# A graph-network layer on one core: GpSimd may fill three pairs of the gather ring ahead in place of four

## The chip, the core and the metric

The kernel runs on one core of a Trainium2 chip. A core has five engines that run side by side, each with its own queue of instructions: TensorE (PE), VectorE (DVE), ScalarE (ACT), GpSimd (POOL) and SyncE (SP, which only starts transfers here), and 16 DMA engines. The metric is device time in microseconds; lower is better.

## What is computed

There are 6250 nodes with 128 values each and 106250 edges, sorted by the node that they lead to. Each edge carries 64 values and one weight. Biases and names are cut to what matters:

```
ef  = relu(edge_attr @ We1 + be1) @ We2 + be2
ef  = ef * sigmoid(edge_weight * Wt + bt)
msg = relu(concat(x[src], ef) @ Wn1 + bn1) @ Wn2 + bn2
out = segment_sum(msg, dst) + x
y   = layernorm(x + out)
```

## The kernel before

**Table.** x[src] @ Wn1[:128] + bn1 needs no edge, so the kernel first makes a table `node_table` of x @ Wn1[:128] + bn1 in DRAM, block by block (13 blocks), and later gathers its rows in place of x's. A gather is an indirect DMA that GpSimd issues: 128 rows of 512 bytes, one for each partition.

**Edges.** 512 edges (4 tiles of 128) are a group, two groups a pair, two pairs a super. There are 104 pairs, numbered from 0. The last matrix product with Wn2 is made after the sum over a node's edges, so each edge costs: a transpose of its attributes (L767), two products (L803, L815), ScalarE's sigmoid (L591) and relu (L599), VectorE's product of the two (L1090), the product with Wn1[128:] (L790), VectorE's addition of the gathered rows (`pre`, L1069), a relu (L535), and a product with a one-hot matrix of the destination nodes (L748) whose result is added to `acc` at L1033.

**Steps.** Each engine works in steps. Step s holds the transposes of pair s, the second layer of pair s - 1, the addition of the gathered rows to pair s - 2 (MSG_LAG), the sums of pair s - 3, and the accumulation of pair s - 4. Some steps also finish a block of 512 nodes (product with Wn2, layer norm, store).

**Gathers.** The rows of pairs 0 to 3 (RAW = 8 groups) are gathered from x itself before the table exists, 32 gathers, into buffers of their own. All later pairs, 4 to 103, use the ring `gathered`: BODY = 4 slots, one pair each, pair p in slot p % 4, eight gathers for each pair, 800 in all. GpSimd starts them once the source ids are spread (`src_e_ready`) and the whole table has landed (`wait_table`, L485). A slot may be filled again when the pair in it has been added: VectorE raises `pre_ready` by one at each addition (L1109). GpSimd runs nothing but these gathers in the main part; its order is the loop at L486. VectorE waits for a pair's landing at L1108, and TensorE at L867 (called at L798, ahead of L803), which makes it wait for the first six gathers of pair s - 2. The last pair's gathers signal one tile at a time (L495), so that its additions can follow each landing.

**Ids.** Pair 7 is the fourth and last pair that fits into the ring before any has been added; pair 8 is the first that must wait at L488.

Of the kernel before, what the change touches and what calls it, by code (L numbers as in the profile page):

```python
# [57 lines left out]
PAIR = 2  # L58
PE2 = PAIR * GE
EF_LAG, MSG_LAG, H_LAG, SUM_LAG, ADD_LAG, SUPER_LAG = 1, 2, 3, 3, 4, 6  # L60
RAW, RAW_BEFORE = 8, 4
# [14 lines left out]
def gnn_kernel(nc, x, src, dst, edge_attr, edge_weight, We1, be1, We2, be2, Wt, bt, Wn1, bn1, Wn2, bn2, out):  # L76
# [6 lines left out]
    BODY = 4  # L83
# [20 lines left out]
    with ExitStack() as ctx:  # L104
# [6 lines left out]
        def sem(name):  # L111
            return ctx.enter_context(nc.semaphore(name))
# [106 lines left out]
        ef_ps, efw_ready, msg_ps, pre_ready, h_ready = (  # L219
            sem(n) for n in ("ef_ps", "efw_ready", "msg_ps", "pre_ready", "h_ready"))  # L220
# [55 lines left out]
        def wait_table(eng):  # L276

            for r, n in enumerate((RING, RING, len(BLOCKS) - 2 * RING)):
                eng.wait_ge(table_out[r], 16 * n)
# [184 lines left out]
        @block.gpsimd  # L464
        def _(pool):
            pool.memset(ident[:, :], 0.0).then_inc(ident_ready, 1)
            pool.wait_ge(ident_ready, 1)
            pool.affine_select(out=ident[:, :], in_=ident[:, :], compare_op=ALU.not_equal, fill=1.0,
                               base=0, pattern=[[-1, P]], channel_multiplier=1).then_inc(ident_ready, 1)
            pool.iota(window_ids[:, :], pattern=[[1, W]], base=0, channel_multiplier=0,  # L470
                      allow_small_or_imprecise_dtypes=True).then_inc(window_ids_ready, 1)
            pool.iota(split_ids[:, :, :], pattern=[[IDS, W1 // IDS], [1, IDS + 1]], base=0, channel_multiplier=0,
                      allow_small_or_imprecise_dtypes=True).then_inc(window_ids_ready, 1)
            pool.memset(zero_c[:, :], 0.0).then_inc(zero_ready, 1)

            def gather_rows(to, rows, index, landed):
                pool.indirect_dma_start(to, None, rows, bass.IndirectOffsetOnAxis(index, 0)).then_inc(landed, 16)  # L477

            for g in range(RAW):
                if g % 2 == 0 and g <= SG:  # L480
                    pool.wait_ge(raw_e_in[g // 2], 16)
                for t in range(TILES):
                    gather_rows(raw_rows[g][:, t * C:(t + 1) * C], x, raw_e[:, g, ORDER[t]:ORDER[t] + 1], raw_in[g])
            pool.wait_ge(src_e_ready, 2)
            wait_table(pool)  # L485
            for p in range(RAW // PAIR, PAIRS):  # L486
                if p >= RAW // PAIR + BODY:
                    pool.wait_ge(pre_ready, p - (BODY - 1))  # L488
                    pool.nop(nofuse=True)
                for q in range(PAIR):  # L490
                    for t in range(TILES):
                        if p < PAIRS - 1:
                            landed = gather_in[p % BODY][0 if q * TILES + t < PART[0] else 1]
                        else:
                            landed = last_gather_in[0 if q == 0 else 1 + t]  # L495
                        gather_rows(gathered[:, p % BODY * PAIR + q, t * C:(t + 1) * C], table,
                                    src_e[:, p * PAIR + q, t:t + 1], landed)
# [901 lines left out]
```

## Time and profile before

| | |
|---|---|
| median of 3 runs | 1063.79 us (1063.65 to 1064.85) |
| span of the profiled execution | 1405.6 us |
| GpSimd busy in it | 787.6 us, 56% |
| TensorE busy in it | 975.4 us, 69% |
| VectorE, ScalarE busy | 651.4 and 582.0 us |
| gathers of the table | 800, 945 ns each on average |

The profile shows one execution, taken while the hardware profiler recorded it. Its span is 32% longer than the timed runs; no separate time of that execution is given besides its span. The page lists for each engine how long it was busy, and for waits what ended them. "remote" and "another core or an unknown queue" mean that the profile has no record of what released the waiting instruction. "issue" means that the engine waited for nothing that the profile shows. A gather's record on GpSimd is the making of its descriptors, not the moving of the data.

### The profile page before, as it was taken

How to read it: one execution, taken by the hardware profiler on the slowest of the kernel's cores; microseconds unless marked ns; L12 is line 12 of the kernel's file. 1: busy time of each engine (PE TensorE's matmuls, PEld its weight loads, DVE VectorE, ACT ScalarE, POOL GpSimd, SP SyncE). 2: the span in 40 equal slices, each digit the busy share in tenths (PEclk: the TensorE clock that was granted, in tenths of full speed). 3: DMA queues.
4: the chain of work that ended last, by engine and by line, in shares of the span. 5: the costliest groups of instructions: out<-in, count | busy, mean ns of one | idle time of the engine just before them, and what ended most of it. 6: DMA issues, size and time to landing. Idle time of an engine off the chain costs nothing.

```text
span 1405.6 us, 15476 instructions
## 1 busy us (share of the span) xinstructions
PE 975.4 (69%) x5031; PEld 704.8 (50%) x5032; DVE 651.4 (46%) x1688; ACT 582.0 (41%) x649; POOL 787.6 (56%) x841
## 2 busy tenths in 40 slices
PE   3547777686776767577578667678576857685775
PEld 3535455454555446455355545555454535453554
DVE  1425444445345445355345534545444535444446
ACT  1325434444444435344244443444344433442442
POOL 7270456655665565566566556556555656655640
PEclk8768978888798888789789888789788888887887
DMA  6433242333323324233242332433323324333310
GB/s 187 144 111 116 85 133 89 124 95 107 120 86 109 116 93 134 87 108 123 85 135 86 109 113 90 124 98 109 118 86 100 126 87 133 96 107 106 98 33 19
DMA packets 70435, 148.44 MB, mean 106 GB/s; under 512 B 17511, under 2 KB 45350, under 8 KB 63686
## 3 DMA queue, kind: packets, MB, share of 16 engines
q1 hardware_dynamic: 41126, 89.26, 18.7%
q0 software_dynamic: 26624, 54.58, 13.6%
q10 hardware_dynamic: 2592, 3.48, 0.7%
q8 instruction: 45, 0.74, 0.2%
q14 instruction: 48, 0.39, 0.1%
HBM read 140.85 MB, written 6.40 MB: 105 GB/s over the span
## 4 chain that ended last, share of the span: by engine, by line
PE 35%; another core or an unknown queue 29%; ACT 19%; issue 12%; DVE 3%; ACTq 1%; DMA 0%; DVEq 0%; SPq 0%
PE psS L748 11%; PE psM L790 8%; ACT tw L591 7%; PE psH L803 7%; PE psE L815 5%; ACT h L535 4%; ACT h L599 2%; ACT eaT L567 1%; ACT found L532 1%; ACT x_sb L612 1%; DVE efw L1090 1%; ACT staged_own L627 1%; PE psS L733 1%; PE psT L767 1%
## 5 line engine op out<-in xcount | busy, mean ns | idle before, releaser
L477 POOL DMA_INDIRECT gathered<-node_table,src_e x800 | 756.2, 945 | 563.8 <-DVE h L1069 284.0
L748 PE MATMUL psS<-onehot,h 128*128 128x128 f32 x1656 | 269.1, 329 | 180.2 <-ACT h L535 154.2
L599 ACT ACTIVATE h<-psH,be_c 128x1024 f32<-128x1024 f32 x104 | 115.8, 1114 | 615.3 <-remote 374.6
L748 PEld LDWEIGHTS psS<-onehot,h 128*128 128x128 f32 x1656 | 251.0, 239 | 199.3 <-issue 126.7
L1069 DVE TENSOR_TENSOR h<-psM,gathered 128x1024 f32<-128x1024 f32 (+1 forms) x104 | 122.7, 1182 | 475.5 <-remote 388.5
L815 PE MATMUL psE<-h,we 128*128 128x512 f32 x416 | 235.3, 687 | 16.4 <-issue 16.1
L790 PE MATMUL psM<-wn,efw 128*128 128x128 f32 x1664 | 227.4, 293 | 21.7 <-issue 15.8
L591 ACT ACTIVATE tw<-ew,bt_c,wt_c 128x1024 f32<-128x1024 f32 x104 | 234.0, 2251 | 7.8 <-DVE efw L1090 3.9
L790 PEld LDWEIGHTS psM<-wn,efw 128*128 128x128 f32 x1664 | 219.0, 211 | 16.1 <-issue 9.7
L1090 DVE SCALAR_TENSOR_TENSOR efw<-psE,be_c,tw 128x1024 f32<-128x1024 f32 x104 | 133.2, 1281 | 127.3 <-PE psE L815 80.3
L803 PE MATMUL psH<-eaT,we 64*128 64x512 f32 x416 | 150.1, 692 | 52.0 <-issue 51.8
L1075 DVE TENSOR_SCALAR onehot<-split_ids,dst_e 128x65 f32<-128x65 f32 x832 | 173.8, 271 | 0.0
L815 PEld LDWEIGHTS psE<-h,we 128*128 128x128 f32 x416 | 79.2, 210 | 164.6 <-issue 164.5
L535 ACT ACTIVATE h<-h 128x1024 f32<-128x1024 f32 (+1 forms) x108 | 110.5, 1026 | 9.9 <-DVE h L1069 9.4
L1083 DVE TENSOR_REDUCE found<-onehot 128x128 f32<-128x512 f32 x104 | 109.8, 1055 | 9.6 <-remote 5.7
L567 ACT ACTIVATE eaT<-psT 128x512 f32<-128x512 f32 x104 | 61.7, 593 | 107.0 <-remote 77.2
L767 PEld LDWEIGHTS psT<-ident,ea 128*128 128x128 f32 x416 | 56.6, 151 | 78.3 <-issue 78.3
L803 PEld LDWEIGHTS psH<-eaT,we 64*128 64x128 f32 x416 | 41.2, 195 | 84.9 <-issue 74.5
L1033 DVE TENSOR_TENSOR acc<-acc,found 128x128 f32 x204 | 58.1, 285 | 48.1 <-issue 31.9
L767 PE MATMUL psT<-ident,ea 128*128 128x128 f32 x416 | 69.5, 288 | 14.8 <-issue 14.8
L733 PE MATMUL psS<-wn,staged_own 128*128 128x128 f32 x88 | 23.0, 351 | 75.2 <-ACT h L535 44.9
L733 PEld LDWEIGHTS psS<-wn,staged_own 128*128 128x128 f32 x88 | 16.6, 236 | 80.6 <-issue 80.6
(111 smaller groups left out, 357.1 us busy)
## 6 DMA issues: line engine op xcount, KB each, us to landing
ew<-in_edge_weight SPq DMA_DIRECT2D x52, 1024.0 KB
ea<-in_edge_attr SPq DMA_DIRECT2D x52, 512.0 KB
gathered<-node_table,src_e POOLq DMA_INDIRECT x800
x_sb<-in_x SPq DMA_DIRECT2D x6, 512.0 KB, 6.3
out_y<-x_sb ACTq DMA_DIRECT2D x12, 256.0 KB
node_table<-gathered SPq DMA_DIRECT2D x7, 256.0 KB, 2.0
node_table<-h SPq DMA_DIRECT2D x4, 256.0 KB
h<-in_x,raw_e POOLq DMA_INDIRECT x16
```

What stands on the lines that cost most here:

```text
L477: pool.indirect_dma_start(to, None, rows, bass.IndirectOffsetOnAxis(index, 0)).then_inc(landed, 16)
L535: return nc.scalar.activation(at, at, ACT.Relu)
L591: nc.scalar.activation(tw[:, s % 2, :].rearrange("c (o i m) -> c o i m", o=2, i=2), ew[s // 2 % 2][:, s % 2 * PAIR:(s % 2 + 1) * PAIR, :] ...
L599: nc.scalar.activation(h1[:, s % 2, :], psH[:, :, :].rearrange("p r e -> p (r e)"), ACT.Relu, bias=be1_c[:, :]).then_inc(h1_ready, 1)
L748: return nc.tensor.matmul(to, h[:, (k - SUM_LAG) % BODY * PAIR + q, t * C:(t + 1) * C], hot, start=(t == 0), stop=(t == TILES - 1))
L767: mm = nc.tensor.transpose(psT[:, (a * PAIR + q) * P:(a * PAIR + q + 1) * P], ea[k // 2][:, k % 2 * PAIR + q, a * P:(a + 1) * P], ident[:, :])
L790: mm = nc.tensor.matmul(psM[:, q, t * P:(t + 1) * P], efw[:, (k - MSG_LAG) % 2, of], wn1[:, 1, :], start=True, stop=True)
L803: mm = nc.tensor.matmul(psH[:, a, :], we1[a * F:(a + 1) * F, :], eaT[a * F:(a + 1) * F, k % 2, :], start=True, stop=True)
L815: mm = nc.tensor.matmul(psE[:, r, :], we2[:, :], h1[:, (k - EF_LAG) % 2, r * GE:(r + 1) * GE], start=True, stop=True)
L1069: return nc.vector.tensor_tensor(to, of, rows, ALU.add)
L1075: made = nc.vector.tensor_scalar(onehot[:, (k - MSG_LAG) % 2, q * TILES + t, :].rearrange("p (a b) -> p a b", b=IDS), split_ids[:, :, 0:ID ...
L1090: nc.vector.scalar_tensor_tensor(efw[:, (k - EF_LAG) % 2, :], psE[:, :, :].rearrange("p r e -> p (r e)"), be2_c[:, :], tw[:, (k - EF_LAG) ...
```

## The change

GpSimd may gather a pair's rows once the pair three in front of it has been added, in place of four. The ring keeps its four slots; one of them less is filled ahead. The first pair that waits is 7 in place of 8.

```
             for p in range(RAW // PAIR, PAIRS):
-                if p >= RAW // PAIR + BODY:
-                    pool.wait_ge(pre_ready, p - (BODY - 1))
+                if p >= RAW // PAIR + BODY - 1:
+                    pool.wait_ge(pre_ready, p - (BODY - 2))
                     pool.nop(nofuse=True)
                 for q in range(PAIR):
                     for t in range(TILES):
```

## Rows read from the trace of the kernel before

**Rows 1.** The page: span, busy us with share and instructions, the chain that ended last.

```profile
span 1405.6 us, 15476 instructions
PE 975.4 (69%) x5031; PEld 704.8 (50%) x5032; DVE 651.4 (46%) x1688; ACT 582.0 (41%) x649; POOL 787.6 (56%) x841
...
by line: another core or an unknown queue 28.7%; issue 12.0%; PE psS L748 10.7%; PE psM L790 8.0%; ACT tw L591 7.4%; PE psH L803 7.0%; PE psE L815 5.2%; ACT h L535 4.5%; ACT h L599 1.8%; ACT eaT L567 1.2%; ACT found L532 1.1%; ACT x_sb L612
```

**Rows 2.** Waits, whole span: engine, line, releaser: us in total, times, longest.

```profile
DVE h L1069 <- remote: 407.9, 68, 19.4
...
POOL gathered L477 <- DVE h L1069: 284.0, 60, 41.8
```

**Rows 3.** GpSimd's gathers: ns min/median/max, first and last start in us.

```profile
L477 POOL DMA_INDIRECT gathered<-node_table,src_e x800: 938/944/1096, 67.3 to 1361.9; - x160
```

**Rows 4.** Timeline, GpSimd: start us, us, instruction, [idle before <- releaser].

```profile
3.10 1.10 POOL L477 DMA_INDIRECT h<-in_x,raw_e  x1 [1.19 <-DMA raw_e<-in_src]
...
41.96 0.94 POOL L477 DMA_INDIRECT raw_own<-in_x,raw_e  x1 [0.30 <-issue]
67.25 0.94 POOL L477 DMA_INDIRECT gathered<-node_table,src_e  x1 [24.36 <-DMA node_table<-gathered]
68.50 0.94 POOL L477 DMA_INDIRECT gathered<-node_table,src_e  x1 [0.30 <-issue]
...
105.95 0.94 POOL L477 DMA_INDIRECT gathered<-node_table,src_e  x1 [0.30 <-issue]
148.73 0.94 POOL L477 DMA_INDIRECT gathered<-node_table,src_e  x1 [41.84 <-DVE h L1069]
```

**Rows 5.** Windows: us, busy of each engine, granted clock, DMA share, GB/s.

```profile
125.00:157.00 32.00, 30.93 (x183) 21.48 (x184) 20.73 (x51) 20.52 (x20) 6.44 (x7) 1.00 0.38 132
148.00:1363.00 1215.00, 867.57 (x4408) 617.72 (x4407) 566.54 (x1468) 518.66 (x563) 725.96 (x768) 0.83 0.33 105
1363.00:1364.00 1.00, 0.00 (x0) 0.00 (x0) 0.00 (x0) 0.88 (x1) 0.00 (x0) 1.00 0.23 66
1364.00:1365.00 1.00, 0.00 (x0) 0.00 (x0) 0.43 (x1) 1.00 (x4) 0.00 (x0) 1.00 0.00 0
```

**Rows 6.** Timeline, the last additions of gathered tiles.

```profile
1391.53 0.48 DVE L1069 TENSOR_TENSOR h<-psM,gathered 128x128 f32<-128x128 f32 x2
```

**Rows 7.** The chain in order of time, to 150 us: start us, us, what.

```profile
13.85 4.72 issue
...
21.78 7.28 another core or an unknown queue
...
30.17 17.82 another core or an unknown queue
...
78.57 5.66 another core or an unknown queue
...
89.18 2.74 another core or an unknown queue
91.97 20.34 another core or an unknown queue
112.34 0.24 DVE h L1069
```

**Rows 8.** Timeline, VectorE: additions to pairs 1 to 4.

```profile
122.18 1.23 DVE L1069 TENSOR_TENSOR h<-psM,h 128x1024 f32<-128x1024 f32 x1 [0.70 <-PE psM L790]
...
131.78 1.21 DVE L1069 TENSOR_TENSOR h<-psM,raw_own 128x1024 f32<-128x1024 f32 x1
...
138.97 1.23 DVE L1069 TENSOR_TENSOR h<-psM,raw_own 128x1024 f32<-128x1024 f32 x1 [0.36 <-PE psM L790]
...
146.76 1.22 DVE L1069 TENSOR_TENSOR h<-psM,gathered 128x1024 f32<-128x1024 f32 x1 [0.52 <-PE psM L790]
```

**Rows 9.** Timeline, VectorE: two additions in the main part.

```profile
1114.47 1.22 DVE L1069 TENSOR_TENSOR h<-psM,gathered 128x1024 f32<-128x1024 f32 x1 [0.18 <-issue]
...
1134.16 1.22 DVE L1069 TENSOR_TENSOR h<-psM,gathered 128x1024 f32<-128x1024 f32 x1 [12.44 <-remote]
```

## Prediction

> **What bounds the kernel now.** I read the page's span and busy table first, then the waits, then GpSimd's instructions in order of time, then the chain. The reader is to see that they do not agree at first sight. No engine is full: TensorE is busy for 69% of the span and GpSimd for 56% [rows 1]. In the waits GpSimd stands 284.0 us in front of L477 until VectorE's add at L1069 releases it, so in the profiled execution it looks like an engine with room to spare. But the largest wait of all, VectorE's 407.9 us at that same add, ends in "remote", work that the profile doesn't name [rows 2], and 29% of the chain that ended last is of that kind [rows 1]. The profiled span is 1405.6 us where the median of the timed runs is 1063.79 us, 341.8 us less. So I do not take the span as the timed run. I ask which engine could still need 1063.8 us once those unnamed waits are gone.
>
> The chain without them is 1405.6 x (1 - 0.287) = 1002 us [rows 1], less than was measured. VectorE, ScalarE and TensorE together, as the chain runs through them, would be done earlier than 1063.8.
>
> GpSimd is different. Its 800 gathers of the table take a median of 944 ns each [rows 3], and the next starts 0.30 us after one has ended; from 67.25 to 105.95 there are 31 pitches [rows 4], 38.70 / 31 = 1.249 us with the rounding of the starts. The 32 raw ones have it too: 3.10 to 41.96, 31 pitches and a slower first one. A pair is eight gathers, 10.0 us. If it never waited, it would start at 3.10 and be done with 832 at 3.1 + 832 x 1.249 = 1042 us. Behind it come the landing of the last rows and the end of the kernel. The DMA engines still move 66 GB/s in the microsecond 1363 to 1364 and nothing in the next, with the last gather's record over at 1361.9 + 0.94 = 1362.8 [rows 3, 5]: 1.2 us. The last two tiles are added from 1391.53 on, and the span ends at 1405.6 [rows 6]: 14.1 us. Together 1042 + 15.3 = 1057.6 us, within 6.2 us of the measured 1063.79. Of the two candidates only GpSimd's issue fills the timed run, and it leaves 6 us for everything else that it waits for. I conclude that the timed kernel is bound by GpSimd's gathers nearly from its start to its end.
>
> **Where GpSimd still waits, and how long.** Twice at the start. It is done with the 32 raw gathers at 42.90 and waits for the table until 67.25 (24.36 us), then fills four pairs of the ring until 106.9 and waits 41.84 us for the first of them to be added, until 148.73 [rows 4]. Both waits lie behind unnamed pieces of the chain: 7.28 and 17.82 us ahead of the table; 5.66, 2.74 and 20.34 us behind it [rows 7]. Taken out, the table is ready at 67.25 - 25.1 = 42.2, so GpSimd goes on as soon as it is free, at some 43.2. Four pairs take it to 43.2 + 32 x 1.249 = 83.2. The first addition of a gathered pair releases it at 148.73 - 53.8 = 94.9, or at 90.2 if the 4.72 us "issue" piece goes too [rows 7]. From there 96 pairs are left: 94.9 + 96 x 8 x 1.249 + 15.3 = 1069.4, or 1064.7 from 90.2. The measured time asks for a release at 1063.8 - 959.2 - 15.3 = 89.3. I take 89.3 to 95, so before the change the wait on the full ring is 6 to 12 us long, not 41.84.
>
> This is the place that decides, so I work out its lower end from the other side. The additions of pairs 1 to 4 start at 122.18, 131.78, 138.97 and 146.76, the last two steps (7.2 and 7.8 us) with TensorE at full granted clock (1.00 over 125 to 157, busy 30.93 of 32 us) [rows 5, 8]. They can't be packed closer. From the table to the addition of pair 0 there are 112.34 - 67.25 = 45.1 us with 28.7 us unnamed, so 16.4 us of named work; then 35.6 us to the end of pair 4's addition (146.76 + 1.22 - 112.34) and 0.8 us to the gather. 42.2 + 16.4 + 35.6 + 0.8 = 95.0. Even if three of the four steps between them were as short as 7.2 us, that is some 6 us less, 89.
>
> **The change, part by part.**
> 1. The test and the number waited for in L487 and L488. For p = 8 to 103 the wait is on a count higher by one; p = 7 waits where it didn't. One more wait instruction of GpSimd's queue: free against a 10 us pair. Nothing but gathers is queued behind it on GpSimd.
> 2. Pair 7's eight gathers move from before the first wait to behind it. Their issue, 8 x 1.249 = 9.99 us, was made while GpSimd would otherwise have stood waiting (83.2 is already their end); the cover was the wait on pair 4. Now three pairs are filled by 43.2 + 24 x 1.249 = 73.2, GpSimd stands until the same 89.3 to 95, and has 97 pairs ahead of it instead of 96. What is late next is each later pair's landing, by one pair. Cost: +9.99 us, if the release at 89.3 or later is past 83.2.
> 3. Slack behind the wait. VectorE at L1069 and TensorE at L799 need pair 7 three steps after the addition of pair 4. Three steps of 7.2 to 9.6 us are 22 to 29 us [rows 8]; eight gathers and their landing are 11.2 us. So nobody waits for pair 7 itself. The consumers then gain about 2.5 us a step on GpSimd (10.0 less 7.5) and catch up with it, after which they wait on landings for the rest.
> 4. The shorter ring in the steady part. GpSimd would be held by it only if a pair's addition came later than two pairs (20 us) after its gathers ended, where it was three pairs (30 us). The widest distance between additions that I saw is 1134.16 - 1114.47 = 19.7 us, and 12.44 us of it are an unnamed wait [rows 9]; without that it is 7.3 us. I count nothing here; the upper bound is below.
> 5. Less traffic before the first addition: 8 gathers of 64 KB move behind it. The bound on both sides: TensorE at full clock has no wait on a transfer in rows 8, so 0; if one of its pieces did depend on it, the 0.5 to 0.7 us waits ahead of those additions are the gain.
>
> Sum against the profiled execution: its consumers are held by the unnamed waits, so its GpSimd waits anyway, and its span should stay near 1405.6, with only the first wait longer by 10 us. Sum against the timed median: 1063.8 + 10.0 = 1073.8 us, +0.94%.
>
> A rule of the skill speaks against this. The rows show GpSimd's track broken by 284.0 us of waits for VectorE and busy for 56% [rows 1, 2]. The Trainium skill, page "Perfetto Trace Analysis", section "What "DMA-bound" means", calls a kernel bound by the DMA sequencer when the issuing engine's track is solid with DMA slices, which it is not here; by that rule an issue slot moved behind a wait would cost nothing, and the sum would be 1063.8. The same skill, page "Trainium Kernel Development and Optimization", section "Best Practices", asks for two buffers to cover transfers, which three slots would satisfy. Both would be right for the profiled execution.
>
> **The rivals.**
> - A, not slower: GpSimd isn't the bound of the timed runs; place: the whole main loop; price 0; time 1063.8. It decides if the consumers need over 8 x 1.249 = 10.0 us a pair in the timed run, or if the gathers' pitch there is below what the consumers' chain needs, (1002 - 95 - 15) / 96 = 9.3 us a pair, 1.16 us a gather. For it: the waits of rows 2, and a mean granted clock below full in the main loop (0.83) [rows 5]. Against it: the consumers' chain is 62 us short of the measured time, GpSimd's only 6 us. Chance 0.14.
> - B, part of it: the release comes before the fourth pair is filled, at 74 to 83; then the loss is the release less 73.2, 1 to 9 us, 1065 to 1072.8. Against it: the lower end worked out above. 0.06.
> - C, more than a slot: the ring of three also holds GpSimd in the steady part. Some steps carry the finishing of a block of nodes (12 of them); if in the timed runs two of them reach past 20 us, each holds GpSimd by some 5 us: 1084. 0.08.
> - D, the change doesn't act or helps: the earlier additions come sooner by the 0.5 to 0.7 us of part 5 and nothing else moves. It would need A as well. Below 1061.7. 0.02.
> - Forecast: one pair's issue, 1073 to 1074.8. 0.70.
>
> **How the numbers follow.** The likeliest is the forecast, 1073.8. About 0.2% (2.1 us) is what a measurement of this kernel can tell from no change. Slower by more: forecast, C and nearly all of B, 0.83. Within it: A and a small part of B, 0.15. Faster: D, 0.02. The range takes in A, B and the forecast with a pitch of 1.16 to 1.264 us (9.3 to 10.1 us a pair) and 2 us for unlike releases: 1063.5 to 1076.
>
> **What would show it.** In the changed kernel's profile: the first ring wait of GpSimd starts after 24 gathers of the table, not 32, and is about 52 us, not 41.84; eight gathers of pair 7 follow the addition of pair 4; the pitch stays 1.25 us; the profiled span stays within some 1% of 1405.6. Step 2 is wrong if the timed runs gain much less than 10 us; then the release came early or GpSimd was not the bound. Step 4 is wrong if they lose over 12 us.

## The result and the profile after

The changed kernel takes 1075.55 us (median; 1072.32 to 1077.79) where the kernel before takes 1064.32 us in the same runs. The ratio is 1.0097, with a 95% interval of 1.0082 to 1.0112. It is slower, by 8.7 to 11.9 us. The forecast was 1073.8 us, +0.94%.

The profiled execution of the changed kernel has nothing of the unnamed waits that filled the one of before. Its span is 1070.5 us, close to the timed runs. The page, its span, its busy table and how the chain that ended last divides:

```profile
span 1070.5 us, 15477 instructions
PE 865.2 (81%) x5031; PEld 628.6 (59%) x5032; DVE 649.8 (61%) x1688; ACT 588.2 (55%) x649; POOL 788.5 (74%) x841
...
POOL 61%; issue 22%; DMA 5%; PE 5%; DVE 4%; ACT 2%; SPq 1%; DVEq 0%; ACTq 0%; POOLq 0%
```

In [rows 1] 29% of the chain was unnamed and TensorE's lines led it. Here GpSimd's gathers are 61% of it, and "issue", mostly the 0.30 us between two gathers, is 22%: the bound that the prediction argued for can be read off directly. GpSimd is busy for 74% and not 100% because those 0.30 us are not counted as busy.

The waits of the same kernel, in the columns of [rows 2]:

```profile
POOL gathered L477 <- issue: 241.4, 792, 0.3
DVE h L1069 <- DMA gathered<-node_table,src_e: 198.3, 66, 7.1
...
POOL gathered L477 <- DVE h L1069: 14.1, 8, 12.0
```

The roles of [rows 2] have changed over. GpSimd stood 284.0 us in front of L477 there, and 14.1 us here, of which one wait is 12.0. VectorE waited for something unnamed there; here it waits 198.3 us for gathers to land, 66 times. The 792 pauses of at most 0.3 us are the fixed distance between gathers.

GpSimd's timeline around its one wait, and two additions of VectorE in the main part:

```profile
72.30 0.94 POOL L477 DMA_INDIRECT gathered<-node_table,src_e  x1 [0.30 <-issue]
85.24 0.94 POOL L477 DMA_INDIRECT gathered<-node_table,src_e  x1 [12.00 <-DVE h L1069]
86.49 0.94 POOL L477 DMA_INDIRECT gathered<-node_table,src_e  x1 [0.30 <-issue]
```

```profile
706.70 1.23 DVE L1069 TENSOR_TENSOR h<-psM,gathered 128x1024 f32<-128x1024 f32 x1 [2.83 <-DMA gathered<-node_table,src_e]
...
718.76 1.23 DVE L1069 TENSOR_TENSOR h<-psM,gathered 128x1024 f32<-128x1024 f32 x1 [5.68 <-DMA gathered<-node_table,src_e]
```

The 24th gather of the table ends at 73.2, and the next starts at 85.24. In [rows 4] it was the 32nd that ended at 106.9, and 148.73 that released the next. But that profile can't be set against this one line by line, since its consumers were held up by waits that are not here. The first experiment gives a profile of the kernel before that can.

### The profile page after: what moved, and what is told of

It reads as the page before. It is cut to its first block, busy times and chain, and to the rows that moved or that the text cites. A ratio compares the mean times of both kernels' runs of the same rounds, so it can differ in the third digit from the quotient of the medians.

```text
span 1070.5 us, 15477 instructions
## 1 busy us (share of the span) xinstructions
PE 865.2 (81%) x5031; PEld 628.6 (59%) x5032; DVE 649.8 (61%) x1688; ACT 588.2 (55%) x649; POOL 788.5 (74%) x841
## 4 chain that ended last, share of the span: by engine, by line
POOL 61%; issue 22%; DMA 5%; PE 5%; DVE 4%; ACT 2%; SPq 1%; DVEq 0%; ACTq 0%; POOLq 0%
POOL gathered L477 61%; DMA gathered<-node_table,src_e 3%; PE psS L748 2%; PE psM L790 1%; DVE h L1069 1%; DMA x_sb<-in_x 1%; DMA ew<-in_edge_weight 1%; ACT tw L591 1%; ACT h L535 1%; PE psH L803 0%; DVE onehot L1075 0%; SPq L400 0%; DVE gathered L943 0%; SPq L406 0%; ACT x_sb L612 0%
## 5 line engine op out<-in xcount | busy, mean ns | idle before, releaser
L477 POOL DMA_INDIRECT gathered<-node_table,src_e x800 | 756.7, 946 | 255.5 <-issue 241.4
L748 PE MATMUL psS<-onehot,h 128*128 128x128 f32 x1656 | 233.5, 298 | 79.8 <-ACT h L535 77.3
L1069 DVE TENSOR_TENSOR h<-psM,gathered 128x1024 f32<-128x1024 f32 (+1 forms) x104 | 122.8, 1183 | 255.8 <-DMA gathered<-node_table,src_e 198.3
L748 PEld LDWEIGHTS psS<-onehot,h 128*128 128x128 f32 x1656 | 215.6, 209 | 98.7 <-issue 52.3
L815 PE MATMUL psE<-h,we 128*128 128x512 f32 x416 | 217.9, 648 | 0.0
L790 PE MATMUL psM<-wn,efw 128*128 128x128 f32 x1664 | 212.4, 283 | 4.8 <-DVE h L1069 4.8
L790 PEld LDWEIGHTS psM<-wn,efw 128*128 128x128 f32 x1664 | 205.1, 201 | 5.6 <-DVE h L1069 5.6
L803 PE MATMUL psH<-eaT,we 64*128 64x512 f32 x416 | 123.6, 672 | 56.0 <-DMA gathered<-node_table,src_e 55.9
L815 PEld LDWEIGHTS psE<-h,we 128*128 128x128 f32 x416 | 74.0, 198 | 135.8 <-issue 135.8
L767 PEld LDWEIGHTS psT<-ident,ea 128*128 128x128 f32 x416 | 53.4, 145 | 56.8 <-issue 56.8
L803 PEld LDWEIGHTS psH<-eaT,we 64*128 64x128 f32 x416 | 32.5, 192 | 70.7 <-DMA gathered<-node_table,src_e 61.9
L767 PE MATMUL psT<-ident,ea 128*128 128x128 f32 x416 | 63.7, 277 | 0.2 <-DMA ea<-in_edge_attr 0.2
L733 PE MATMUL psS<-wn,staged_own 128*128 128x128 f32 x88 | 21.2, 327 | 40.8 <-ACT h L535 40.8
```

Source lines behind the costliest of these rows:

```text
L748: return nc.tensor.matmul(to, h[:, (k - SUM_LAG) % BODY * PAIR + q, t * C:(t + 1) * C], hot, start=(t == 0), stop=(t == TILES - 1))
L767: mm = nc.tensor.transpose(psT[:, (a * PAIR + q) * P:(a * PAIR + q + 1) * P], ea[k // 2][:, k % 2 * PAIR + q, a * P:(a + 1) * P], ident[:, :])
L790: mm = nc.tensor.matmul(psM[:, q, t * P:(t + 1) * P], efw[:, (k - MSG_LAG) % 2, of], wn1[:, 1, :], start=True, stop=True)
L803: mm = nc.tensor.matmul(psH[:, a, :], we1[a * F:(a + 1) * F, :], eaT[a * F:(a + 1) * F, k % 2, :], start=True, stop=True)
L815: mm = nc.tensor.matmul(psE[:, r, :], we2[:, :], h1[:, (k - EF_LAG) % 2, r * GE:(r + 1) * GE], start=True, stop=True)
L1069: return nc.vector.tensor_tensor(to, of, rows, ALU.add)
```

## Experiments

### The kernel before once more

No edit.

> The kernel before, unchanged, to see a profile of it without the unnamed waits. Theory (GpSimd's issue is the bound, its only ring wait is the first one): 1064 us; GpSimd starts the gathers of the table at some 43.6, has filled four pairs at 83.3, is released at some 85.2 as in the changed kernel's profile, so waits 2 us and not 41.84, and then issues 96 pairs at 10.0 us. Rival (the profiled execution of before is typical of the timed ones): a span near 1400 us in the profile again, and 60 waits of GpSimd for VectorE.

Measured: 1064.19 us, ratio to before 0.9996 (0.9983 to 1.0009), profiled span 1061.6 us. Its GpSimd timeline at the first wait, and its waits:

```profile
82.18 0.95 POOL L477 DMA_INDIRECT gathered<-node_table,src_e  x1 [0.30 <-issue]
84.89 0.94 POOL L477 DMA_INDIRECT gathered<-node_table,src_e  x1 [1.77 <-DVE h L1069]
86.14 0.94 POOL L477 DMA_INDIRECT gathered<-node_table,src_e  x1 [0.31 <-issue]
```

```profile
DVE h L1069 <- DMA gathered<-node_table,src_e: 197.7, 65, 5.6
...
POOL gathered L477 <- DVE h L1069: 3.9, 8, 1.8
```

This is the same place in the kernel before. GpSimd has filled four pairs at 83.1, waits 1.77 us, and is released at 84.89, 0.35 us from the 85.24 of the changed kernel. So the release did not move by more than that, and the one wait grew from 1.77 to 12.00 us: 10.23 us, of which eight pitches of 1.25 us are 10.0. The profile ahead of the prediction was of an exceptional execution. What held its engines in it stays open: of the ten profiles taken after it, of these kernels and of variants, none shows a wait that ends in "remote".

### Only the first wait

```
-                if p >= RAW // PAIR + BODY:
-                    pool.wait_ge(pre_ready, p - (BODY - 1))
+                if p >= RAW // PAIR + BODY - 1:
+                    pool.wait_ge(pre_ready, max(p - (BODY - 1), RAW // PAIR + 1))
```

> Only pair 7 waits for pair 4's addition; pairs 8 to 103 keep the wait on the pair four in front. Theory (the loss is pair 7's issue, moved out of the first wait): all of the loss, +8 to +10 us, about 1073 us, with a first wait of 12.0 us. Rival (the ring of three holds GpSimd in the steady part): less than the change loses, in the extreme 1064 us.

Measured: 1075.57 us, ratio 1.0083 (1.0056 to 1.0111), so +8.8 us by the ratio and +10.9 by the medians. Within these intervals that is the whole loss of the change, with the full depth of the ring for pairs 8 to 103. Its waits and its one long wait in the timeline:

```profile
POOL gathered L477 <- DVE h L1069: 13.8, 7, 12.0
```

```profile
85.59 0.94 POOL L477 DMA_INDIRECT gathered<-node_table,src_e  x1 [12.00 <-DVE h L1069]
```

### Only the later waits

```
                 if p >= RAW // PAIR + BODY:
-                    pool.wait_ge(pre_ready, p - (BODY - 1))
+                    pool.wait_ge(pre_ready, p - (BODY - 2))
```

> The other half: pair 7 is gathered freely as before, pairs 8 to 103 wait for the pair three in front. Theory: pair 8 then waits for pair 5's addition, which ends one step of 7.2 us later than pair 4's, so GpSimd is held at 83.3 until 92.4 in place of 85.2: +7.2 us, about 1071.5 us, with one wait of 9.2 us at the start and none to speak of later. Rival (the steady part costs nothing and neither does the start): 1064 us. Rival (the steady part costs by itself): over 1073 us, with waits spread over the main part.

Measured: 1071.03 us, ratio 1.0066 (1.0041 to 1.0090), so +7.0 us by the ratio and +6.4 by the medians, where +7.2 was worked out.

```profile
82.07 0.94 POOL L477 DMA_INDIRECT gathered<-node_table,src_e  x1 [0.30 <-issue]
92.50 0.94 POOL L477 DMA_INDIRECT gathered<-node_table,src_e  x1 [9.49 <-DVE h L1069]
```

```profile
POOL gathered L477 <- DVE h L1069: 12.2, 10, 9.5
```

Pair 8 now waits for pair 5, one step later: 92.50 in place of 84.89, 7.6 us. The total of all its waits for VectorE is 12.2 us, and 9.49 of it are this one. The ring of three costs nothing behind it. The two halves of the change lengthen the first wait by 10.2 and 7.7 us, but together by 10.2, not 17.9: both are the same wait, entered or left at different points. They can't be added.

### Two pairs ahead

```
-                if p >= RAW // PAIR + BODY:
-                    pool.wait_ge(pre_ready, p - (BODY - 1))
+                if p >= RAW // PAIR + BODY - 2:
+                    pool.wait_ge(pre_ready, p - (BODY - 3))
```

> One slot less again: GpSimd may gather a pair once the pair two in front has been added. Theory: the first wait begins after 16 gathers, at 63.3, and ends at the same 85.2, so 98 pairs are left: another +10.0 us over the changed kernel, about 1084 us, as long as a pair's addition ends within 10 us of the end of its gathers. Additions ended 2 to 8 us after it in the changed kernel's profile, so a few waits of 1 to 3 us may come on top: 1084 to 1100 us. Rival (the loss is a fixed price of the first wait or of the earlier wait instruction): about 1074 us.

Measured: 1085.52 us, ratio 1.0198 (1.0160 to 1.0235), +21.1 us by the ratio, +20.9 by the medians, and about twice the change's loss.

```profile
62.29 0.94 POOL L477 DMA_INDIRECT gathered<-node_table,src_e  x1 [0.30 <-issue]
86.23 0.94 POOL L477 DMA_INDIRECT gathered<-node_table,src_e  x1 [23.00 <-DVE h L1069]
```

```profile
POOL gathered L477 <- DVE h L1069: 28.5, 19, 23.0
```

A second slot costs a second pair's issue. The wait is 23.0 us: 20 us more than before are the issue of two pairs, and 1.3 us come from the release, which lies at 86.23 in this execution and not at 84.89. The 5.5 us that are left of 28.5 are spread over 18 others of 0.3 us each, the ordinary distance. Even a ring of two does not hold GpSimd in the main part.

The spans of the profiled executions follow from one sum. All five kernels issue 800 gathers of the table; they differ by the one wait:

| kernel | wait, us | wait less 1.77 | span less 1061.6 | timed median less before's |
|---|---|---|---|---|
| before, once more | 1.77 | | | -0.5 |
| changed | 12.00 | 10.2 | 8.9 | 11.2 |
| only pair 7 | 12.00 | 10.2 | 12.1 | 10.9 |
| only later | 9.49 | 7.7 | 7.2 | 6.4 |
| two ahead | 23.00 | 21.2 | 21.2 | 20.9 |

What is left between the wait and the span, up to 2 us, lies in the pitch and in the end of the kernel. Behind the wait the pitch is (1045.5 - 84.89) / 767 = 1.2524 us in the kernel before and (1054.5 - 85.24) / 775 = 1.2507 us in the changed one; 768 times the difference is 1.3 us. In the kernel with only pair 7 the last gather starts at 1056.7, which makes its pitch 1.2530 us, and its end, from that start on, is 17.0 us where the kernel before has 16.1.

```profile
L477 POOL DMA_INDIRECT gathered<-node_table,src_e x800: 940/944/1415, 43.5 to 1045.5; - x160
```

```profile
L477 POOL DMA_INDIRECT gathered<-node_table,src_e x800: 940/944/1397, 43.6 to 1054.5; - x160
```

The first row is of the kernel before, the second of the changed one.

### Fewer gathers: where is the next bound?

The number of gathers left out was put into the loop, and the counts that L1108 and L867 wait for were lowered with it:

```
+LEFT_OUT = 1
+LANDED = (PART[0] - LEFT_OUT, PART[1])
...
                     for t in range(TILES):
+                        if p < PAIRS - 1 and q * TILES + t < LEFT_OUT:
+                            continue
```

> The kernel before with one gather of each pair's eight left out for pairs 4 to 102 (the first tile of the even group, so its rows are stale), everything else the same. Theory (GpSimd's issue is the bound): four pairs are filled at 43.6 + 28 x 1.249 = 78.6, released at 85.2; (95 x 7 + 8) x 1.249 = 840.6 us of issue and 15.1 us of end follow: 941 us plus 2 us around the span. Rival A (the engines that use the rows are the bound): near 1064 us.

Measured: 950.34 us, ratio 0.8925 (0.8909 to 0.8941), 7 us above the 943 that the theory gave and 114 us below the kernel before. Of the kernel with one gather left out (its line numbers are 2 to 4 higher), GpSimd's gathers and the waits for them:

```profile
L479 POOL DMA_INDIRECT gathered<-node_table,src_e x701: 941/947/1348, 43.5 to 929.3; - x176
```

```profile
DVE h L1073 <- DMA gathered<-node_table,src_e: 26.5, 21, 4.8
POOL gathered L479 <- DVE h L1073: 11.7, 13, 8.0
```

GpSimd still waits only once for long, 8.0 us. The 99 gathers less are worth 99 x 1.25 = 124 us. Of the 10 us that were not gained, 6.3 lie in the first wait, 8.03 us in place of 1.77, since four of the gathers left out were issued ahead of it and the release came at 86.51. Another 3.5 lie in the end behind the last gather, which has grown from 15.2 to 948.9 - 929.3 - 0.9 = 18.7 us. And VectorE's waits for landings have shrunk from 198 us to 26.5: the consumers are now nearly as slow as the gathers. That the end is longer because the consumers are further behind is argued only.

The same with LEFT_OUT = 2:

> Two of each pair's eight gathers left out for pairs 4 to 102 (the first two tiles of the even group). GpSimd alone would need 85.2 + (95 x 6 + 8) x 1.249 + 15.1 = 822 us. TensorE's step took 7.2 to 7.8 us at full clock without the finishing of blocks, so its chain is 85 + 99 x 7.5 + 15 = 843 us and some 2 to 4 us more for each of 12 blocks: 870 to 890 us, and GpSimd should now wait for VectorE all through the main part. Theory: 860 to 900 us, bound by TensorE's chain. Rival: 1064 us if the gathers never were the bound, 824 us if TensorE's chain is shorter than I think.

Measured: 939.83 us, ratio 0.8828 (0.8813 to 0.8844). The bound has changed over, as the theory had it: no wait of VectorE for a landing is left, and TensorE leads the chain that ended last, where GpSimd had 63% of it in the kernel before:

```profile
PE 65%; ACT 12%; issue 9%; DVE 7%; DMA 3%; ACTq 2%; DVEq 1%; SPq 1%
```

But the time is 40 us above the 900 of the theory. My 7.5 us a step had left out that the steps are not alike; these additions follow each other at 7.2 to 10.6 us:

```profile
514.23 1.22 DVE L1073 TENSOR_TENSOR h<-psM,gathered 128x1024 f32<-128x1024 f32 x1
522.52 1.23 DVE L1073 TENSOR_TENSOR h<-psM,gathered 128x1024 f32<-128x1024 f32 x1 [2.87 <-PE psM L794]
529.74 1.23 DVE L1073 TENSOR_TENSOR h<-psM,gathered 128x1024 f32<-128x1024 f32 x1
536.97 1.22 DVE L1073 TENSOR_TENSOR h<-psM,gathered 128x1024 f32<-128x1024 f32 x1
547.59 1.22 DVE L1073 TENSOR_TENSOR h<-psM,gathered 128x1024 f32<-128x1024 f32 x1 [2.07 <-PE psM L794]
```

```profile
POOL gathered L479 <- DVE h L1073: 121.9, 59, 14.3
```

From 503.95 to 598.13 there are eleven steps in that timeline, 8.6 us each. The first ten steps after pair 4's addition take 7.4 us on average (85.69 to 159.91), and the eight from 529.74 to 598.13 take 68.4 us, some 9 us more than eight at that pace. One block of nodes is finished in them, its product with Wn2 in the two steps from 536.97 to 556.25, and 2 to 4 us had been expected for a block. That the block accounts for all of the 9 us is argued only.

And the same edit on top of the change, three pairs ahead:

> The same two gathers of each pair left out, with the change: three pairs ahead. Theory: GpSimd now has 2 us and more to spare in each pair, so pair 7's issue is hidden again and the change costs nothing: the time of the kernel with two left out, within 3 us. Rival (the change costs by the depth of the ring, whoever is the bound): slower by the issue of a pair, 7.5 us, or more.

Measured: 946.15 us (937.16 to 948.78, 4 runs), ratio 0.8901 (0.8879 to 0.8923). That is 6.3 us over its partner's median, outside the 3 us of the theory, and the two intervals do not overlap, so by these runs the rival was ahead; but the profiled spans stand the other way round, 935.4 us with three ahead and 943.2 us with four. The medians alone don't settle it, and I made another pair with more room for GpSimd.

LEFT_OUT = 3, four and three pairs ahead:

> The kernel before with three of each pair's eight gathers left out for pairs 4 to 102 (the first three tiles of the even group). GpSimd alone would need 85 + (95 x 5 + 8) x 1.249 + 15 = 703 us. Theory: with two left out TensorE's chain was already the bound at 940 us, so nothing more is gained: 935 to 942 us. Rival (the rows' traffic or GpSimd's issue still set the time with two left out): some 100 us less, 820 to 840 us.

> The same three gathers left out, with the change: three pairs ahead. Theory: the change costs nothing where GpSimd has room; the time of the kernel with three left out, within 3 us. Rival (the 6 us between the two kernels with two gathers left out are a real price of the shorter ring): 5 us or more slower again.

Measured: 941.12 us (ratio 0.8820, 0.8796 to 0.8844) with four ahead, 938.49 us (ratio 0.8808, 0.8784 to 0.8832) with three. The waits, first with four ahead, then with three:

```profile
POOL gathered L479 <- DVE h L1073: 253.5, 96, 16.8
```

```profile
POOL gathered L479 <- DVE h L1073: 256.2, 95, 24.1
```

A third gather less brought nothing (939.8 and 941.1 us), so the consumers' chain of some 940 us is the bound from there on, and not the rows' traffic. The change costs nothing there that these runs can tell, although the first wait is 7.3 us longer: 24.1 in place of 16.8. Pair 7's five gathers are 6.2 us of this, and a release 1.1 us later (86.03 and 84.97) is the rest. GpSimd has over 250 us of waits in which to give them back.

The 6 us of the pair before did not come back, and the granted clock of the single runs says where they lie. In the 22 runs of these four kernels the time goes with TensorE's mean granted clock:

| mean granted clock of the run | runs | time, us |
|---|---|---|
| 0.970 to 0.974 | 12 | 937.07 to 940.62 |
| 0.968 and 0.969 | 3 | 940.66 to 941.99 |
| 0.964 to 0.966 | 5 | 944.54 to 945.40 |
| 0.962 | 2 | 947.76 and 948.78 |

With two gathers left out, three of the four runs with three pairs ahead have 0.966 or less, and two of the six with four ahead. At the same clock the two agree: 944.54 us with three ahead and 945.13 us with four, both at 0.966; 937.16 and 938.25 us, both at 0.972. So at an equal clock no price of the shorter ring is seen. Why the clock differs from run to run is open, and four runs can't exclude that the change had a part in it there; with three gathers left out the kernel with three ahead has no lower clock than its partner (0.966 to 0.974 against 0.964 to 0.974).

## Why the prediction was right, step by step

**The bound.** Right. The prediction set two sums against the measured time: GpSimd's own, 1057.6 us, and the rest of the chain without its unnamed pieces, 1002 us. GpSimd fills the time, as the pages after and the kernel with one gather left out show. The second sum was some 60 us too long; the chain of the consumers is about 940 us. With three gathers left out the additions of pairs 4 to 102 follow each other at (916.11 - 82.99) / 98 = 8.5 us. So the point at which rival A would decide, put at 9.3 us a pair or 1.16 us a gather, is really some 8.5 us a pair, 1.06 us a gather.

In the page after, GpSimd is busy for only 74% of the span, yet its track is closed apart from a fixed 0.30 us behind each gather. The Trainium skill, page "Perfetto Trace Analysis", section "What "DMA-bound" means", speaks of a DMA sequencer as the bound where the issuing engine's track is solid with DMA slices. Read by the busy share it would not name GpSimd here; the 114 us gained with one gather of eight left out decide that GpSimd is the bound all the same.

**The release.** The time of it was mis-sized. It came at 84.9 us, not at 89.3 to 95, and GpSimd started the table's gathers at 43.5 (43.2 had been worked out). The additions in the kernel before, once more:

```profile
51.50 1.22 DVE L1069 TENSOR_TENSOR h<-psM,h 128x1024 f32<-128x1024 f32 x1
59.18 1.22 DVE L1069 TENSOR_TENSOR h<-psM,h 128x1024 f32<-128x1024 f32 x1
67.79 1.22 DVE L1069 TENSOR_TENSOR h<-psM,raw_own 128x1024 f32<-128x1024 f32 x1
75.15 1.23 DVE L1069 TENSOR_TENSOR h<-psM,raw_own 128x1024 f32<-128x1024 f32 x1 [0.36 <-PE psM L790]
82.92 1.23 DVE L1069 TENSOR_TENSOR h<-psM,gathered 128x1024 f32<-128x1024 f32 x1 [0.51 <-PE psM L790]
```

From pair 0's addition to the release there are 84.89 - 51.50 = 33.4 us, where 36.4 had been taken from [rows 8]: the two steps that I had left as they stood, 9.8 and 9.6 us, are 7.7 and 8.6 here. The other 7 us put pair 0's addition at 51.50 and not at 42.2 + 16.4 = 58.6, and they lie ahead of the table. TensorE's first product at L815 starts at 41.69 here and at 73.71 in the profile ahead of the prediction, 32.0 us earlier, where 25.1 had been taken out. From there to pair 0's addition it is 9.8 us here and 38.6 - 28.7 = 9.9 us there, so what was taken out behind the table was right. Ahead of it, taking out only the pieces that the chain calls unnamed was too little: there was the 4.72 us "issue" piece, which the prediction priced but left in the upper end, and the granted clock was 0.62 from 20 to 48 us where it is 1.00 from 20 to 43.5 here. How the 7 us divide between the two is not shown.

It did not change the answer, but the margin was small. A release at any time past 83.2 gives the same 10.0 us, and 84.9 is 1.7 us past it. With a release 2 us earlier rival B would have begun. The lower end of 89 was given as safe, and it was not. In the nine profiles in which pair 4's addition releases GpSimd, the release lies from 84.89 to 87.66, never before 83.2; that the forecast held is in part owed to this small margin.

**Part 2, the moved issue.** Right, and it is the whole effect: 9.99 us worked out, 10.23 us in the traces, and the same from the waits of pair 7 alone. The timed loss of 8.7 to 11.9 us agrees.

**Part 3, slack behind the wait.** Right. Pair 7, the eighth addition, is added at 106.09 without a wait for its rows. The six steps from pair 4's addition at 83.27 to pair 10's at 127.45 take 7.4 us each, 2.6 us less than a pair's gathers, where 2.5 had been worked out. The first of VectorE's waits for a landing is pair 11's:

```profile
106.09 1.21 DVE L1069 TENSOR_TENSOR h<-psM,gathered 128x1024 f32<-128x1024 f32 x1
...
139.74 1.22 DVE L1069 TENSOR_TENSOR h<-psM,gathered 128x1024 f32<-128x1024 f32 x1 [3.86 <-DMA gathered<-node_table,src_e]
```

**Part 4, the ring in the steady part (rival C).** Right to count nothing. Neither the kernel with only the later waits nor the one with two pairs ahead has a second long wait. The allowance of 20 us was ample.

**Part 1 and part 5.** Nothing to be seen of either: the release moved by 0.35 us, the other way from the gain of 0.5 to 0.7 that part 5 allowed for, and by less than the 2.8 us by which it differs between the profiles.

**The profiled span.** The forecast that it would stay near 1405.6 us failed with its premise, that the unnamed waits come with being profiled. They didn't come back. The first wait was to be 52 us and was 12.0, by the same shift of 10 us.

**The scatter.** The change's four runs lie from 1072.32 to 1077.79 us, no wider than the kernel before itself, whose 15 runs beside the first experiments lie from 1062.10 to 1068.28. Here the time does not go with the granted clock: the fastest and the slowest of the four have 0.939 and 0.943. The pitch, multiplied by 800, and the release could make 2 to 3 us of the scatter; the runs that were not profiled show neither, so this is argued only.

No version beats the kernel before. A fifth slot was not tried; by the wait of 1.77 us that is left in the profile it could take away that much, less than these runs can tell.

## What to carry to other kernels

A ring's depth is not only cover against late landings. Where the engine that fills it is the bound, each slot is also work done before the first release, and one slot less costs that slot's whole issue time once, however loose the ring is afterwards, as long as the first release comes after the slot would have been filled. To find such a bound in a profile that is much longer than the timed runs, add up each engine's own chain with its fixed pauses and see which one fills the measured time; a busy share of 56% may be a full engine. And see how far the cover reaches before calling an effect safe: here the fourth slot was full only 1.8 us before the release, and with an earlier release the loss would have been smaller.

## What was new of the hardware

Gathers of 128 rows by 512 bytes, where GpSimd waited for nothing but the last one, started 1.250 to 1.253 us apart in the kernels with 800 of them, whether the DMA engines moved 106 GB/s on average (the profile ahead of the prediction) or 140 (the same kernel once more); 0.94 to 0.95 us of it is the record and 0.30 us a pause in which nothing is shown.

One execution of a kernel on a single core can be a third longer than all the others, 1405.6 us against 1062 to 1068, with TensorE's granted clock at 0.82 in place of 0.94 on average and no releaser named for the waits; its cause is open.

And where TensorE's chain was the bound, the single runs of one kernel differed by up to 1.2% (937.16 to 948.78 us), and the time went with the mean granted clock of the run (0.972 to 0.962).
